# Adaptive projection and Hadamard-quantised feed-forward on one core: written-out start and end, weights in quarters, loop with other lags

## The chip, the core and the metric

The kernel runs on one core of a Trainium2 chip. The time is the device time of one execution in microseconds, and for the kernel before it is the median of three executions, 296.42 us (293.67 to 298.29). The engines are named as the profile names them: PE is TensorE, PEld its weight loads, DVE is VectorE, ACT is ScalarE, POOL is GpSimd, and SP is SyncE, which only issues transfers here. PEq, ACTq and POOLq are the sequencers of those engines.

## What is computed

Sixty-four samples of 64 x 512 are multiplied with a matrix that is picked from 200 by an index. A feed-forward block with ternary weights then runs on the result, and is added to the input. `fwht` is the normalised Walsh-Hadamard transform along the last axis.

```python
def cond(x, conditions, weights):
    return einsum('bct,bcd->bdt', x, weights[conditions])

def act_quant(x):                      # 8 bits, one scale per token
    scale = 127 / clip(max(abs(x), axis=-1, keepdims=True), 1e-5, None)
    return clip(round(x * scale), -127, 127) / scale

def weight_quant(w):                   # ternary, one scale per matrix
    scale = clip(mean(abs(w)), 1e-5, None)
    return clip(round(w / scale), -1, 1) * scale

def hbitlinear(x, w):
    return einsum('bsd,fd->bsf', act_quant(fwht(x)), weight_quant(w))

def reference(x, idx, w_cond, w_up, w_down):
    h = hbitlinear(cond(x, idx, w_cond), w_up)     # 512 -> 1024
    return x + hbitlinear(square(relu(h)), w_down) # 1024 -> 512
```

## The kernel before, in words

Two samples fill the 128 partitions (a pair), and two pairs make a tile, so there are 16 tiles of 256 tokens. All work is written in stages, each a small function of a tile t (and of a half h, k, u or v of it), with its own semaphore waits. For one tile they follow one another like this; the engine stands in brackets.

- `x_outer` [POOL, L340]: the outermost step of the Hadamard transform of x, two halves. `project` [PE, L528]: eight small matmuls with the picked matrices, into the one buffer `y_ps`. `y_high` [ACT, L417] and `y_low` [DVE, L669] split the result in two parts for exact arithmetic.
- `had_z` [PE, L543]: the rest of the transform, into the one buffer `z_ps`. `z_absmax`, `z_floor`, `z_invert` [DVE, L674 to L686] make the scale, `quant_z` [ACT, L423] rounds, `turn_z` [a DMA transpose issued by ACT, L432] turns the tile, and `keep_z` [POOL, L347] keeps the scales.
- `up` [PE, L561], four parts u into two buffers `h_ps`; `relu` [ACT, L439] for each, `square` [ACT, L446] for each pair.
- `g_outer` and `g_inner` [DVE, L693 and L699], two instructions each: two steps of the second transform, SBUF to SBUF. `p_high` [ACT, L452] and `p_low_pool` [POOL, L373] split the result.
- `had_u` [PE, L576], k = 0 and 1, both into the one buffer `u_ps`, so that k = 1 waits until k = 0 has been read. `token_units` [POOL, L352 to L366] works out `kappa`, the floor that `u_floor` needs; `u_absmax`, `u_floor`, `u_invert` [DVE, L713 to L726] make the scale; `quant_u` [ACT, L457] rounds; `turn_u` [DMA transpose from ACT, L464] turns.
- `down` [PE, L586]; `u_unscale` [POOL, L381]; `residual` [DVE, L732] adds x; a store per half.

The order of the work is set by hand. Each engine has a list `step`, in which `run(stage, lag, ...)` means: in step s do this stage for tile s - lag. PE's and DVE's lists reach a lag of 7, ACT's and POOL's a lag of 6. `run_steps` writes the first ten (ACT and POOL: eight) steps out, then loops over two steps at a time up to step 15, and ends with steps in which the stages of tiles past 15 are dropped. So the end of the program keeps the order of the loop.

The weights are prepared in the first steps, by `once(s, stage, ...)`. SP issues the loads, each matrix in two halves, between the loads of x and the gathers of the picked matrices. `weight_abs` sums absolute values, one half on DVE (L624) and one on ACT (L403); `weight_sum` [PE, L504] and `weight_scale` [DVE, L630 to L643] make the scale. Then for each quarter of a matrix: `weight_rint` [ACT, L410] rounds by adding a large constant, `weight_clip` [DVE, L650] limits to -1, 0, 1, `weight_turn` [PE, L515] transposes the low bf16 halves in eight matmuls, `weight_evac` [DVE, L662] takes the constant off while it copies from PSUM. Each gather (L270) waits for POOL's memset of the whole of `w_diag` (L326).

## Time and profile before

| | us |
|---|---|
| median of three executions | 296.42 |
| lowest, highest | 293.67, 298.29 |
| the profiled execution | 297.55 |
| its span, first to last instruction | 295.7 |
| busy: PE, DVE, ACT, POOL | 254.3, 245.7, 185.0, 168.3 |
| mean granted clock of PE, as a share of 2.4 GHz | 0.975 |

The times in the rows below count from the start of the span. Matmuls overlap one another, so the start of one stage to the start of the next tells more of PE than its busy time does.

### The profile page before, as it was taken

The numbers are of one execution on the slowest core, as the hardware profiler recorded it, in microseconds if no ns is written. First come the engines' busy times: TensorE is split into PE (matmuls) and PEld (weight loads), VectorE is DVE, ScalarE is ACT, GpSimd is POOL, SyncE is SP. The second block draws the span as 40 slices with busy tenths as digits, with TensorE's granted clock in tenths as the row PEclk, the third lists the DMA queues.
The fourth block names the chain that finished last, engine by engine and source line by source line (L and its number), as shares of the span: only waits on it lengthen the run. The fifth ranks groups of instructions, "written<-read, shape, count | busy, mean of one in ns | idle before, by whom it ended". The sixth has DMA issues, their size and how long they took to land.

```text
span 295.7 us, 6449 instructions
## 1 busy us (share of the span) xinstructions
PE 254.3 (86%) x1864; PEld 209.1 (71%) x1864; DVE 245.7 (83%) x346; ACT 185.0 (63%) x237; POOL 168.3 (57%) x200
## 2 busy tenths in 40 slices
PE   0277998979899899999899989998999999967863
PEld 0267888859688688888788878887887777635531
DVE  1168799999999988999999999999989898795451
ACT  1068677758577767675867576767676765924310
POOL 8034433595858686656595659574946548474400
PEclk9999899999999999999999999999999999995996
DMA  5585441235385946465664342433343434323262
GB/s 201 206 312 201 121 114 38 88 99 141 98 170 141 162 132 114 144 97 152 104 165 94 90 87 90 88 89 71 106 88 91 90 108 125 64 80 71 92 144 84
DMA packets 67049, 35.16 MB, mean 119 GB/s; under 512 B 57170, under 2 KB 57170, under 8 KB 67026
## 3 DMA queue, kind: packets, MB, share of 16 engines
q10 hardware_dynamic: 51200, 12.59, 24.3%
q1 hardware_dynamic: 15826, 22.29, 22.6%
q8 instruction: 11, 0.18, 0.3%
q14 instruction: 12, 0.10, 0.1%
HBM read 13.89 MB, written 8.39 MB: 75 GB/s over the span
## 4 chain that ended last, share of the span: by engine, by line
DVE 24%; PE 21%; POOL 19%; issue 18%; DMA 6%; ACT 6%; ACTq 2%; SPq 2%; POOLq 1%; DVEq 1%
PE u_ps L576 8%; POOL p_lo L373 8%; DVE g L699 5%; PE o_ps L586 5%; POOL x_half L340 4%; DMA uqT<-uq 4%; DVE u_max L713 3%; PE h_ps L561 3%; PE z_ps L543 3%; POOL u_deq L381 3%; DVE g L693 3%; DVE x_all L650 3%; DVE out_sb L732 2%; DVE z_max L674 2%; ACT uq L457 2%
## 5 line engine op out<-in xcount | busy, mean ns | idle before, releaser
L373 POOL TENSOR_TENSOR p_lo<-g,p_hi 128x1024 fp32r<-128x1024 f32 x32 | 82.8, 2608 | 59.3 <-ACT p_hi L452 51.8
L576 PE MATMUL u_ps<-had_r,p_hi 128*128 128x256 f32 x256 | 65.6, 293 | 11.8 <-ACT uq L457 11.5
L561 PE MATMUL h_ps<-zqT,w_upT 128*128 128x256 f16 x512 | 66.7, 273 | 2.5 <-ACT g L439 2.5
L693 DVE TENSOR_TENSOR g<-g 128x1024 f32<-128x1024 f32 x32 | 66.9, 2099 | 0.2 <-issue 0.2
L586 PE MATMUL o_ps<-w_downT,uqT 128*128 128x512 f16 x256 | 62.2, 387 | 5.1 <-DMA uqT<-uq 4.5
L576 PE MATMUL u_ps<-had_r,p_lo 128*128 128x256 f32 x256 | 63.9, 286 | 0.0
L576 PEld LDWEIGHTS u_ps<-had_r,p_hi 128*128 128x128 f32 x256 | 49.8, 195 | 16.5 <-issue 14.7
L340 POOL TENSOR_TENSOR x_half<-x_all 128x512 f32<-128x512 f32 (+1 forms) x32 | 43.5, 1361 | 21.2 <-DMA x_all<-in_x_dram 14.9
L561 PEld LDWEIGHTS h_ps<-zqT,w_upT 128*128 128x128 f16 x512 | 47.6, 98 | 10.4 <-issue 3.1
L439 ACT ACTIVATE g<-h_ps 128x512 f32<-128x512 f32 x64 | 36.5, 596 | 27.0 <-PE h_ps L561 13.0
L528 PE MATMUL y_ps<-w_diag,x_half 128*128 128x128 f32 (+1 forms) x256 | 38.5, 299 | 15.4 <-DMA w_diag<-in_L_cond_weights_dram 11.1
L713 DVE TENSOR_REDUCE u_max<-u_ps 128x1 f32<-128x1024 f32 x32 | 38.9, 1217 | 13.8 <-PE u_ps L576 13.8
L528 PEld LDWEIGHTS y_ps<-w_diag,x_half 128*128 128x128 f32 x256 | 36.3, 211 | 19.4 <-issue 15.9
L576 PEld LDWEIGHTS u_ps<-had_r,p_lo 128*128 128x128 f32 x256 | 50.0, 195 | 0.0
L699 DVE TENSOR_TENSOR g<-g 128x1024 f32<-128x1024 f32 x32 | 47.1, 1511 | 0.0
L586 PEld LDWEIGHTS o_ps<-w_downT,uqT 128*128 128x128 f16 x256 | 24.7, 99 | 30.9 <-DMA uqT<-uq 5.4
L457 ACT ACTIVATE uq<-u_ps,u_mul 128x1024 f16<-128x1024 f32 x32 | 35.5, 1109 | 17.5 <-DVE u_mul L726 17.4
L452 ACT ACTIVATE p_hi<-g 128x1024 fp32r<-128x1024 f32 x32 | 33.7, 1052 | 8.9 <-DVE g L699 7.8
L423 ACT ACTIVATE zq<-z_ps,z_col 128x512 f16<-128x512 f32 x32 | 22.0, 687 | 26.1 <-DVE z_col L686 25.5
L543 PE MATMUL z_ps<-had_r,y_hi 128*128 128x256 f32 x128 | 34.9, 304 | 2.5 <-ACT zq L423 2.5
L446 ACT ACTIVATE g<-g 128x1024 f32<-128x1024 f32 x32 | 33.6, 1051 | 1.9 <-ACT g L439 0.4
L543 PE MATMUL z_ps<-had_r,y_lo 128*128 128x256 f32 x128 | 33.2, 290 | 0.0
(42 smaller groups left out, 252.8 us busy)
## 6 DMA issues: line engine op xcount, KB each, us to landing
x_all<-in_x_dram SPq DMA_DIRECT2D x16, 512.0 KB, 4.2
out_dram<-out_sb SPq DMA_DIRECT2D x32, 256.0 KB, 2.0
x_all<-in_L_ffn_w_up_dram SPq DMA_DIRECT2D x2, 1024.0 KB, 7.1
x_all<-in_L_ffn_w_down_dram SPq DMA_DIRECT2D x2, 1024.0 KB, 5.9
w_diag<-in_L_cond_weights_dram SPq DMA_DIRECT2D x64, 16.0 KB, 2.4
zqT<-zq ACTq DMA_TRANSPOSE x32, 3.1
uqT<-uq ACTq DMA_TRANSPOSE x32, 3.1
x_all<-in_hadamard_dram SPq DMA_DIRECT2D x1, 256.0 KB, 3.6
```

The lines of the kernel that those rows point to most:

```text
L340: nc.gpsimd.tensor_tensor(x_half[h][:, :, :], xt[:, :, 0, :], xt[:, :, 1, :], (ALU.add, ALU.subtract)[h]).then_inc(s_xh[h], 1)
L373: nc.gpsimd.tensor_tensor(p_lo[par][:, :, i], g[par][:, :, i], p_hi[par][:, :, i].bitcast(FP32), ALU.subtract).then_inc(s_plo[k], 1)
L439: nc.scalar.activation(g[par][:, 2 * u:2 * u + 2, :], h_ps[u % 2][:, :, :], ACT.Relu)\
L457: nc.scalar.activation(uq[k][:, :], u_ps[:, :], ACT.Copy, scale=u_mul[:, k:k + 1])\
L528: mm = nc.tensor.matmul(y_ps[:, l, j * P:(j + 1) * P], x_half[h][:, j, l * P:(l + 1) * P], w_diag[:, bass.ds(t * KP + j, 1), :].rearrange( ...
L543: mm = nc.tensor.matmul(z_ps[:, blk * 256:(blk + 1) * 256], part[par][:, 2 * blk + i, k * P:(k + 1) * P], had_r[:, i, :], start=(i == 0 an ...
L561: mm = nc.tensor.matmul(h_ps[u % 2][:, i, :], w_upT[:, q, f * P:(f + 1) * P], zqT[par][:, q, :], start=(q == 0), stop=(q == TC - 1))
L576: mm = nc.tensor.matmul(u_ps[:, blk * 256:(blk + 1) * 256], part[par][:, 2 * blk + i, k * P:(k + 1) * P], had_r[:, i, :], start=(i == 0 an ...
L586: mm = nc.tensor.matmul(o_ps[k][:, :], uqT[par][k][:, m, :], w_downT[:, m, :], start=(m == 0), stop=(m == FC - 1))
L693: nc.vector.tensor_tensor(g2[:, n, :, :], g[par][:, 0:4, :], g[par][:, 4:8, :], (ALU.add, ALU.subtract)[n]).then_inc(s_g2, 1)
L699: nc.vector.tensor_tensor(p4[par][:, :, n, :], g2[:, :, 0:2, :].rearrange("p h a n -> p h (a n)"), g2[:, :, 2:4, :].rearrange("p h a n -> ...
L713: nc.vector.tensor_reduce(u_max[:, k:k + 1], u_ps[:, :], AX.X, ALU.max, apply_absolute_value=True).then_inc(s_umax[k], 1)
```

## The change

The loop body is reordered on every engine. `once` is gone: `begin(at)` writes out, instruction by instruction, what each engine does before step 5, and `finish(at)` what it does after step 15. The last stages come one step sooner (`down` and `residual` with lag 6), and `up` and `relu` for u = 0 and 1 come with lag 2 in place of 3.

```diff
-            first = (lags + 3) // 2 * 2
-            for s in range(first):
-                step(stages_of(s // 2, s % 2, s), once_in(s))
+            begin(at)
+            first = (lags + 3) // 2 * 2
+            for s in range(BEGIN, first):
+                step(stages_of(s // 2, s % 2, s))
             with eng.Fori(first // 2, TILES // 2) as half:
...
-            for s in range(TILES, TILES + lags):
-                step(stages_of(s // 2, s % 2, s), once_in(s))
+            finish(at)
```

PE's list for a step in the loop, which the prediction goes through:

```diff
-            def step(run, once):
-                run(up, 3, 1)
-                run(down, 7, 1)
-                run(project, 0, 0)
-                run(up, 3, 0)
-                run(had_z, 1, 0)
-                run(had_u, 5, 0)
-                run(up, 3, 2)
-                run(down, 6, 0)
-                run(project, 0, 1)
-                run(up, 3, 3)
-                run(had_u, 5, 1)
-                run(had_z, 1, 1)
+            def step(run):
+                run(down, 6, 0)
+                run(had_u, 5, 0)
+                run(had_z, 1, 0)
+                run(project, 0, 0)
+                run(up, 3, 3)
+                run(down, 6, 1)
+                run(up, 3, 2)
+                run(had_u, 5, 1)
+                run(project, 0, 1)
+                run(up, 2, 0)
+                run(had_z, 1, 1)
+                run(up, 2, 1)
```

PE's written-out start, its first lines, and its whole written-out end, which the prediction adds up:

```diff
+            def begin(at):
+                at(project, 0, 0)
+                at(project, 0, 1)
+                weight_sum(0)
+                at(had_z, 0, 0)
+                at(project, 1, 0)
+                weight_turn(0, 0)
...
+            def finish(at):
+                at(had_u, 11, 0)
+                at(up, 13, 3)
+                at(down, 10, 0)
+                at(had_z, 15, 0)
+                at(up, 13, 2)
+                at(had_u, 11, 1)
+                at(down, 10, 1)
+                at(up, 14, 1)
+                at(up, 14, 0)
+                at(had_u, 12, 0)
+                at(down, 11, 0)
+                at(had_z, 15, 1)
+                at(had_u, 12, 1)
+                at(up, 14, 2)
+                at(up, 14, 3)
+                at(down, 11, 1)
+                at(had_u, 13, 0)
+                at(up, 15, 1)
+                at(up, 15, 0)
+                at(down, 12, 0)
+                at(up, 15, 3)
+                at(up, 15, 2)
+                at(had_u, 13, 1)
+                at(down, 12, 1)
+                at(had_u, 14, 0)
+                at(down, 13, 0)
+                at(had_u, 14, 1)
+                at(down, 13, 1)
+                at(had_u, 15, 0)
+                at(had_u, 15, 1)
...
```

The weights: the up matrix is loaded by ACT's queue, together with the Hadamard matrix, and both matrices come in quarters. The absolute sums are taken by quarters. The rounding writes fp16 straight (the scale is kept 2^24 times larger, so that the values are whole multiples of the smallest fp16 number), and the clip is done by the instruction that empties PSUM. `relu` multiplies the factor back.

```diff
-            def weight_rint(n, u):
+            def weight_round(n, u):
                 act.wait_ge(s_winv[n], 1)
-                part = w_raw[n][:, u * WQ:(u + 1) * WQ]
-                nc.scalar.activation(part, part, ACT.Copy, scale=w_inv[:, n:n + 1], bias=RINT)\
-                    .then_inc(s_wrint[n], 1)
+                nc.scalar.activation(w_int[n][u], w_raw[n][:, u * WQ:(u + 1) * WQ], ACT.Copy,
+                                     scale=w_inv[:, n:n + 1]).then_inc(s_wrint[n], 1)
-            def weight_clip(n, u):
-                dve.wait_ge(s_wrint[n], u + 1)
-                part = w_raw[n][:, u * WQ:(u + 1) * WQ]
-                nc.vector.tensor_scalar(part, part, RINT + 1.0, RINT - 1.0, ALU.min, ALU.max)\
-                    .then_inc(s_wclip[n], 1)
...
-                nc.vector.tensor_scalar(dst, src, float(-BIAS16), None, ALU.add).then_inc(s_wT[n], 1)
+                nc.vector.tensor_scalar(dst, src, UNIT, -UNIT, ALU.min, ALU.max).then_inc(s_wT[n], 1)
```

SP's issues at the start, and POOL's memset, of which only the part of the first two tiles now stands ahead of the first gathers:

```diff
             load_x(0, 0)
-            sp.dma_start(had_f, had).then_inc(s_had, 16)
-            load_weight(0, 0)
             gather_w(0, 0)
-            load_weight(0, 1)
             load_x(0, 1)
             gather_w(0, 1)
-            load_weight(1, 0)
-            load_weight(1, 1)
+            for u in range(4):
+                load_w_down(u)
...
+            act.dma_start(had_f, had).then_inc(s_had, 16)
+            for u in range(4):
+                load_w_up(u)
...
-            nc.gpsimd.memset(w_diag[:, :, :], 0.0).then_inc(s_zero, 1)
+            nc.gpsimd.memset(w_diag[:, 0:2 * KP, :], 0.0).then_inc(s_zero, 1)
...
+            nc.gpsimd.memset(w_diag[:, 2 * KP:PAIRS, :], 0.0).then_inc(s_zero, 1)
```

Three places of the new order. First ACT at its start: what stood there in the kernel before, and what stands there now.

```order
L417 ACT_TABLE_LOAD
L417 ACTIVATE y_hi<-y_ps 128x512
L403 ACTIVATE x_all,w_abs<-x_all 128x2048
L417 ACTIVATE y_hi<-y_ps 128x512
L410 ACTIVATE x_all<-x_all,w_inv 128x1024 x2
L417 ACTIVATE y_hi<-y_ps 128x512
L410 ACTIVATE x_all<-x_all,w_inv 128x1024 x2
```

```order
L509 DMA x_all<-in_hadamard_dram 128x512
L438 DMA x_all<-in_L_ffn_w_up_dram 128x2x512 x4
L459 ACT_TABLE_LOAD
L459 ACTIVATE y_hi<-y_ps 128x512
L446 ACTIVATE x_all,w_abs<-x_all 128x1024 x2
L459 ACTIVATE y_hi<-y_ps 128x512
L452 ACTIVATE x_all<-x_all,w_inv 128x1024 x2
L465 ACTIVATE zq<-z_ps,z_col 128x512
L459 ACTIVATE y_hi<-y_ps 128x512
```

Five DMA issues now stand ahead of ACT's first work, and the first rounding for a token (`zq`) comes right behind the first two quarters. Next DVE in one step of the loop, from the `y_low` of half 1 on: before, and now.

```order
L669 TENSOR_TENSOR y_lo<-y_ps,y_hi 128x512
L713 TENSOR_REDUCE u_max<-u_ps 128x1
L674 TENSOR_REDUCE z_max<-z_ps 128x1
L720 TENSOR_SCALAR u_abs<-u_max,kappa 128x1
L680 TENSOR_SCALAR z_col<-z_max 128x1
L726 RECIPROCAL u_mul<-u_abs 128x1
L732 SCALAR_TENSOR_TENSOR out_sb<-o_ps,u_deq,x_all 128x512
L686 RECIPROCAL z_col<-z_col 128x1
L693 TENSOR_TENSOR g<-g 128x1024
L732 SCALAR_TENSOR_TENSOR out_sb<-o_ps,u_deq,x_all 128x512
L693 TENSOR_TENSOR g<-g 128x1024
```

```order
L869 TENSOR_TENSOR y_lo<-y_ps,y_hi 128x512
L886 RECIPROCAL z_col<-z_col 128x1
L893 TENSOR_TENSOR g<-g 128x1024 x2
L913 TENSOR_REDUCE u_max<-u_ps 128x1
L920 TENSOR_SCALAR u_abs<-u_max,kappa 128x1
L926 RECIPROCAL u_mul<-u_abs 128x1
L899 TENSOR_TENSOR g<-g 128x2x512 x2
L869 TENSOR_TENSOR y_lo<-y_ps,y_hi 128x512
```

All four instructions on `g` now stand close together, with one `u_absmax`, `u_floor`, `u_invert` between them, and both residuals come later. Last ACT at the end of the program, from the `p_high` of tile 14, k = 1, on: before, and now.

```order
L452 ACTIVATE p_hi<-g 128x8x128
L457 ACTIVATE uq<-u_ps,u_mul 128x1024 x2
L464 DMA_TRANSPOSE uqT<-uq 128x8x128
L452 ACTIVATE p_hi<-g 128x8x128
L464 DMA_TRANSPOSE uqT<-uq 128x8x128
L452 ACTIVATE p_hi<-g 128x8x128
L457 ACTIVATE uq<-u_ps,u_mul 128x1024 x2
L464 DMA_TRANSPOSE uqT<-uq 128x8x128 x2
L457 ACTIVATE uq<-u_ps,u_mul 128x1024
L464 DMA_TRANSPOSE uqT<-uq 128x8x128
```

```order
L495 ACTIVATE p_hi<-g 128x8x128
L500 ACTIVATE uq<-u_ps,u_mul 128x1024
L507 DMA_TRANSPOSE uqT<-uq 128x8x128
L495 ACTIVATE p_hi<-g 128x8x128
L500 ACTIVATE uq<-u_ps,u_mul 128x1024
L507 DMA_TRANSPOSE uqT<-uq 128x8x128 x2
L495 ACTIVATE p_hi<-g 128x8x128
L500 ACTIVATE uq<-u_ps,u_mul 128x1024
L507 DMA_TRANSPOSE uqT<-uq 128x8x128
L500 ACTIVATE uq<-u_ps,u_mul 128x1024
L507 DMA_TRANSPOSE uqT<-uq 128x8x128
```

The `p_high` of tile 15 (the second and third `p_hi` rows of each) stood behind the `quant_u` of tile 14, k = 0; now its first half stands ahead of the `quant_u` of tile 14, k = 1, and its second half ahead of the first of tile 15 only.

## Rows read from the trace of the kernel before

**Rows 1.** Stretches: length; busy PE, PEld, DVE, ACT, POOL; PE's clock; DMA share.

```profile
0.00:20.00 20.00, 5.64 (x22) 4.97 (x23) 5.43 (x9) 5.63 (x7) 9.42 (x12) 1.00 0.63 221
20.00:40.00 20.00, 17.90 (x130) 16.65 (x130) 16.81 (x29) 14.77 (x19) 7.59 (x7) 0.91 0.62 198
40.00:60.00 20.00, 18.25 (x171) 16.51 (x170) 19.58 (x30) 14.85 (x22) 8.14 (x6) 1.00 0.22 57
...
72.60:223.60 151.00, 146.25 (x1114) 122.50 (x1115) 141.95 (x200) 107.17 (x141) 102.91 (x120) 1.00 0.51 116
223.60:296.00 72.40, 56.08 (x352) 39.48 (x351) 49.58 (x65) 33.25 (x39) 31.48 (x48) 0.92 0.38 94
```

**Rows 2.** Instructions in order of time, first 23 us; start, length, engine, idle before.

```profile
0.70 3.51 POOL L326 MEMSET w_diag<- 128x4096 f32 x1 [0.29 <-POOLq L802]
...
5.21 4.43 SPq L270 DMA_DIRECT2D w_diag<-in_L_cond_weights_dram  x4
...
11.12 2.04 PE L528 MATMUL y_ps<-w_diag,x_half 128*128 128x128 f32 x8 [11.12 <-DMA w_diag<-in_L_cond_weights_dram]
...
14.67 2.05 PE L528 MATMUL y_ps<-w_diag,x_half 128*128 128x128 f32 x8 [1.50 <-DVE y_lo L669]
...
15.66 1.91 ACT L403 ACTIVATE x_all<-x_all 128x2048 bf16<-128x2048 f32 x1 [1.86 <-DMA x_all<-in_L_ffn_w_up_dram]
...
22.29 0.56 PE L543 MATMUL z_ps<-had_r,y_hi 128*128 128x256 f32 x1
```

**Rows 3.** Groups by line and shape: count, busy, mean ns, idle before.

```profile
L373 POOL TENSOR_TENSOR p_lo<-g,p_hi 128x1024 fp32r<-128x1024 f32 x32 | 82.8, 2608 | 59.3 <-ACT p_hi L452 51.8 <-PE u_ps L576 7.5
...
L650 DVE TENSOR_SCALAR x_all<-x_all 128x1024 f32<-128x1024 f32 x8 | 9.2, 1163 | 0.4 <-ACT x_all L410 0.4
```

**Rows 4.** PE in order of time: `up` for tile 2, tile 3 and tile 13.

```profile
56.69 1.04 PE L561 MATMUL h_ps<-zqT,w_upT 128*128 128x256 f16 x8
...
71.56 1.04 PE L561 MATMUL h_ps<-zqT,w_upT 128*128 128x256 f16 x8
...
222.56 1.04 PE L561 MATMUL h_ps<-zqT,w_upT 128*128 128x256 f16 x8
```

**Rows 5.** The chain that ended last, one step of the loop (200 to 222 us).

```profile
202.27 2.14 PE u_ps L576 x16
204.41 0.96 PE z_ps L543 x8
205.37 0.89 PE h_ps L561 x8
206.26 1.73 PE o_ps L586 x8
...
217.01 2.15 PE u_ps L576 x16
```

**Rows 6.** The same chain, 57 to 72 us: start, length, what.

```profile
57.76 3.39 POOL p_lo L373
...
65.25 3.30 DVE g L699 x2
...
68.57 1.07 ACT p_hi L452
...
72.03 3.39 POOL p_lo L373
```

**Rows 7.** DVE in order of time, at 192 us.

```profile
192.20 3.28 DVE L693 TENSOR_TENSOR g<-g 128x1024 f32<-128x1024 f32 x1
```

**Rows 8.** The chain again, 256 to 296 us.

```profile
268.25 3.75 PE u_ps L576 x16
...
275.01 2.16 PE u_ps L576 x16
...
280.16 2.16 PE u_ps L576 x16
...
285.26 4.64 DMA uqT<-uq
```

510 lines of the change are left out of this document (387 added, 123 removed).

## Prediction

> **What bounds the kernel now.** I read the stretches first. Between 72.6 and 223.6 us PE is busy for 146.25 of 151.0 us and DVE for 141.95, both at the full clock (1.00 of 2.4 GHz), while ACT and POOL have a third of their time left [rows 1]. So there are three kernels in one. There is a start in which little runs, with PE at 5.64 of the first 20 us. There is a middle that PE nearly fills. And there is an end, from 223.6 us on, with PE at 56.08 of 72.4 us and a clock of 0.92. Next the chain that ended last, inside one step of the loop: it stays on PE from 202.27 to 217.01, which is 14.74 us for the twelve stages of a step, one behind the other with no gap [rows 5]. In plain stages that is had_u 1.92 to 2.14, had_z 0.96, up 0.88, down 1.73 and, by subtraction, project 0.89. Ten steps take from 72.6 to 223.6 us (the second `up` of tile 3 ends at 72.6, that of tile 13 at 223.6 [rows 4]), or 15.10 us each. In the loop the most that any order can win is therefore about 0.4 us a step, unless PE's own work shrinks, and it doesn't: the same matmuls are issued.
>
> At the start the chain is a different one. The first gather is issued at 5.21, behind a memset that ends at 4.21, and the first project starts at 11.12 [rows 2]. DVE is busy for 19.58 of the 20 us between 40 and 60 [rows 1]. In the tail I looked for where PE stands still between one had_u and the next, since these share one buffer.
>
> **The change part by part.** The sum is made against the profiled execution, 297.55 us with a span of 295.7, so 1.85 us lie outside the span. It was 1.13 us slower than the median.
>
> *First gather.* The memset ahead of it shrinks to an eighth (about 0.45 of 3.51 us), so the first gather waits for the load of the indices, whose landing no row shows. Before, it came 1.0 us after the memset's end. It can come at 2.2 if the indices are as early as the shorter memset (0.70 + 0.45, and the same 1.0, together), and at 5.21 if they are what it waited for all along. I put it at the middle, 3.7. Four gathers take 4.43 us to issue as before, and the first project would start 1.5 us sooner. Against that, 2 MB of up weights now run beside the gathers from the start, where one half of them was issued only after the gathers. I take 1.0 us of gain (bounds -1 and +3) and start project at 10.1.
> The skill has a rule against this part. The Trainium skill, "DMA: Bandwidth & Descriptors", section "Issuing engines are not separate DMA queues", says that transfers issued by different engines run on the same 16 DMA engines and interleave, and that only sequencer time is saved. Rows 1 show a DMA share of 0.63 over the first 20 us. By that rule alone this part would be worth 0 and the result 1 us later.
>
> *From the first project to the first had_z.* Before, that is 11.12 to 22.29, or 11.2 us [rows 2]. ACT's absolute sum of half a matrix, from 15.66 on, stands ahead of the second y_high, and a third project and the first weight transposes stand ahead of had_z. Now had_z is behind two projects and one tiny matmul. From one project to the next, with y_high and y_low between, it is 14.67 - 11.12 = 3.55 us [rows 2], so two of them make 7.1. had_z starts at 17.2, 5.1 us sooner. The quarter sums on ACT fit inside the wait for the second project.
>
> *The weights.* The clips go: 9.2 us of DVE [rows 3]. They lay where DVE had 36.4 of 40 us busy. The rounding, the transposes and the emptying of PSUM stay, the absolute sums cost the same in more pieces. With DVE relieved, ACT is late next. It was busy for 35.3 us in the first 60 [rows 1]; take off the table load and add 0.6 for four more pieces, and some 34.6 us of it must lie between the first y_high at 12.2 and the last relu ahead of step 5. In 20 to 60 us ACT stood idle for 10.4 of 40; I allow 8 for the shorter stretch. That puts the end of `begin` at 12.2 + 34.6 + 8 = 54.8. Before, the same point is 57.7 (end of the second `up` of tile 2 [rows 4]) plus two weight transposes that are still to come, 58.9. Step 5 has no `down` yet, so PE's content is 14.5 - 3.5 = 11.1; with 0.9 of waits both ups of tile 3 are done at 66.8 to 67.0, against 72.6. Start and step 5 together: 5.6 us gained. The bounds are 1 (only the first gather helps, ACT eats the rest) and 10 (DVE's 9.2 us come through in full).
>
> *The loop.* Ten steps at 15.10. PE's floor is 14.5 to 14.7. The order of PE's list leaves 5.3 us of other stages between the two had_u of a tile, both ways round, where u_absmax, floor, invert, quant_u and their gaps need 280.16 - 275.01 - 2.16 = 2.99 us [rows 8]. So the wait for uq ahead of had_u should go. What may take its place is a ring, visible in rows 6: p_lo ends at 61.15, then POOL's x_half, scales and kappa, then u_floor, g_inner at 65.25 for 3.30, p_hi for 1.07, and two p_lo up to 75.4. The new order has the same ring, with token_units behind one x_outer and both u_unscale on POOL, and u_floor ahead of g_inner on DVE. From the end of one p_low pair to the end of the next I get 4.10 + 3.30 + 1.07 + two gaps of 0.1 + 2 x 2.61 (the mean of p_lo [rows 3]) = 13.9, below 15.1 but not far below. turn_u for k = 0 is issued late in ACT's list, behind both p_high, and down for k = 0 is now PE's first stage of the next step; that leaves about 1 us of slack. I take 15.0 a step, 1.0 us gained over ten, with bounds of 14.7 (4 gained) and 16.0 (9 lost).
> One g_outer takes 3.28 us where p_lo runs beside it [rows 7], and where only short work runs on POOL two g instructions take 3.30 together [rows 6]. The Trainium skill, "SBUF — State Buffer", section "SBUF: two separate sides", says why: a DVE instruction with two SBUF inputs and a GpSimd one that reads SBUF take one port pair in turn, each for its whole length. In the new order the g instructions are early in the step and the p_low pair late, so g meets x_outer instead; by that rule it then waits for at most two x_outer a step. This is the reason why I don't put the loop slower.
>
> *The tail.* At the end of step 15 both kernels have done the same PE work (had_u to tile 10, down to tile 9, ups 0 and 1 of tile 13), so the tails compare from 223.6 on. Before: 295.7 - 223.6 = 72.1 us. After: the had_u run through one buffer, and from one start to the next takes at least 5.15 us (275.01 to 280.16 [rows 8], 2.16 for the matmuls and 2.99 until the buffer has been read). From PE's new list, with 2.0 for had_u itself: 11/0 to 11/1 carries two ups, a down and a had_z, 6.45; then 5.5, 5.15, 5.5, 7.25 (four ups and a down), and four times 5.15. The sum from had_u 11/0 to had_u 15/1 is 50.45. The last had_u to the end of the span was 295.7 - 280.16 = 15.54 and is the same chain in the new order (its transpose alone 4.64 [rows 8]). Together 66.0. I add 1.0 for g and p_lo meeting somewhere: 67.0, a gain of 5.1. What goes is the block at 268.25, where had_u took 3.75 us instead of 2.16 [rows 8]; PE had stood still ahead of it, and the granted clock of the tail is 0.92 [rows 1], so part of it ran at 1.2 GHz instead of 2.4. In the order of before, ACT waits there for the scale of tile 14 with p_high of tile 15 behind it. Bounds: 0 (each wait comes back elsewhere) and 6.5.
>
> *Sum.* 5.6 + 1.0 + 5.1 = 11.7 us. Span 284.0, execution 285.85, and 1.13 less for the median: 284.7 us.
>
> **The rivals.**
> *More than forecast.* The loop runs at PE's content, 14.7 (4 us instead of 1), and the DVE relief comes through, 8 instead of 5.6. For it: DVE is the fullest engine from 40 to 60 us, at 98%, and ACT has a quarter of that time left. Against it: ACT's sum above. Time 284.7 - 3 - 2.4 = 279.3.
> *The start gives little.* ACT is the bound there, its transposes are issued between its own work, and PE catches up on nothing; the tail gives half. 1 + 0 + 2.5 = 3.5 gained: 292.9.
> *Slower: the ring kappa, g_inner, p_high, p_low closes.* If the p_low pair and one g_inner are at their long lengths (2 x 3.39 and 3.28 + 1.65, half of the 3.30), it is 4.10 + 4.93 + 1.07 + 0.2 + 6.78 = 17.1 us a step if that happens in each, and about a half less above 15.1 if in every other. It decides from 15.1 on. I price it at 16.6, where it costs 1.5 us times ten, 15 us, against 10.7 gained at the ends: 296.4 + 4.3 = 300.7. For it: this ring is on the chain already. Against it: p_low no longer meets g.
> *It doesn't do what it says.* The ends wait for landings (the last transpose, 4.64 us, the gathers), which no order shortens; this is the second rival with 0 from the tail as well, and is counted in it.
>
> **How the numbers follow.** Forecast 0.58, more 0.20, little 0.15, slower 0.07. The forecast's own range is 280 to 289. I take the whole range from 275 to 292. Faster than 290.5 is over 2% faster, which is about what a measurement of this kernel can tell from no change: nearly all of the first, all of the second, a fifth of the third, 0.80. Slower by over 2% (302.3) is half of the ring's case at most, 0.04. The rest, 0.16, is within 2%.
>
> **What would show it.** First project near 10.1 and first had_z near 17.2; ACT over 80% busy from 20 to 50 us; ups of tile 3 done by 67; steps of 15.0; had_u starts in the tail 5.15 apart for the last five, at full clock. The forecast is wrong if steps take over 15.5, if p_lo again meets g in the loop, or if the stretch between had_u 13/1 and 15/0 has PE waiting for p_lo.

## The result and the profile after

| us | before | changed |
|---|---|---|
| median (executions) | 295.62 (4) | 311.6 (4) |
| lowest, highest | 293.67, 298.29 | 308.4, 314.84 |
| profiled execution, its span | 297.55, 295.7 | 308.4, 306.3 |
| start, to the second `up` of tile 3 | 72.6 | 69.35 |
| ten steps of the loop | 151.0 | 156.1 |
| tail | 72.1 | 80.8 |

The changed kernel is slower: the ratio is 1.0484, with a 95% interval of 1.0349 to 1.062. The forecast was 284.7 us, so the prediction was wrong by 27 us and in the sign. Start, loop and tail came out at 69.4, 156.1 and 80.8 us where 67.0, 150 and 67.0 were forecast. The start is better than before and the other two parts are worse. Some executions are slow ones, among them two of the four of the changed kernel (314.84 and 313.08 us), and the ratios and the gains below leave them out, so that the gains count from 309.26 us, the median of the other two (308.4 and 310.11), and not from 311.6.

The profiled execution of the kernel before took 297.55 us, where the medians of the later comparisons are 294.8 to 295.12. In its start the granted clock is 0.91 between 20 and 40 us [rows 1]. In the trace of experiment 3, which has the same start, it is 1.00 there, and the second `up` of tile 3 ends at 71.28 instead of 72.6. So of the 3.2 us by which the start seems better, about 1.3 belong to that one execution.

The stretches of the changed kernel, with the columns of [rows 1] (length; busy PE, PEld, DVE, ACT, POOL; PE's granted clock; DMA share; GB/s). The first three are start, loop and tail. The others are the single steps of the loop, cut where `down` of k = 0 starts on PE.

```profile
0.00:69.40 69.40, 48.90 (x389) 45.21 (x390) 40.34 (x77) 44.21 (x62) 32.77 (x34) 0.98 0.53 161
69.40:225.50 156.10, 147.32 (x1121) 122.90 (x1121) 131.71 (x199) 105.15 (x141) 110.04 (x121) 0.99 0.53 108
225.50:306.30 80.80, 58.66 (x354) 41.33 (x352) 47.08 (x68) 34.20 (x40) 31.57 (x48) 0.91 0.35 88
...
84.08:98.58 14.50, 14.50 (x113) 12.30 (x113) 13.81 (x20) 10.64 (x15) 11.82 (x13) 1.00 0.59 135
98.58:114.60 16.02, 14.66 (x115) 12.20 (x112) 13.63 (x21) 10.89 (x16) 11.95 (x15) 1.00 0.61 121
114.60:133.21 18.61, 16.34 (x115) 12.74 (x113) 12.68 (x21) 10.54 (x15) 10.65 (x13) 0.91 0.61 103
133.21:150.84 17.63, 14.64 (x114) 12.19 (x112) 12.69 (x20) 10.52 (x15) 10.98 (x13) 1.00 0.66 108
150.84:167.60 16.76, 14.66 (x114) 12.20 (x112) 12.68 (x21) 10.53 (x15) 10.65 (x13) 1.00 0.67 114
167.60:182.09 14.49, 14.49 (x114) 12.29 (x112) 12.68 (x21) 10.53 (x15) 10.52 (x13) 1.00 0.44 91
```

Read down the length. Some steps take 14.49 or 14.50 us, and in those PE is busy for all of it. Four steps in the middle take 16.02 to 18.61 us, and PE's busy time does not explain them (14.64 to 14.66 in three, 16.34 in the one where the clock was 0.91). DVE, ACT and POOL did no more work there than in the steps around them. So this is a wait that comes and goes. The DMA share stands out: 0.61 to 0.67 in the slow steps, and 0.44 in the first quick one behind them, though 0.59 in the quick one ahead. The share alone does not decide it.

The page's groups tell what PE waited for. These are busy time and mean ns of one, then the idle time ahead and what ended it.

```profile
L366 POOL TENSOR_TENSOR p_lo<-g,p_hi 128x1024 fp32r<-128x1024 f32 x32 | 75.3, 2368 | 71.7 <-ACT p_hi L495 71.6
L705 PE MATMUL h_ps<-zqT,w_upT 128*128 128x256 f16 x512 | 70.0, 285 | 10.2 <-issue 9.6
...
L730 PE MATMUL o_ps<-w_downT,uqT 128*128 128x512 f16 x256 | 62.6, 390 | 11.9 <-DMA uqT<-uq 10.9
...
L893 DVE TENSOR_TENSOR g<-g 128x1024 f32<-128x1024 f32 x32 | 40.4, 1297 | 2.3 <-ACT g L489 1.4
```

`down` stood for 10.9 us because the transposed `uq` had not landed, and `up` for 9.6 us. Meanwhile the part of the change that takes load off DVE did work: `g_outer` (L893) takes 1297 ns in the mean, where its mean before was 2099 (L693) and one beside p_lo took 3.28 us [rows 7], and p_lo itself is at 2368 ns against 2608 [rows 3].

**The loop.** First what SP issues around one slow step, 98 to 107.5 us: start, length of the issue, queue, transfer.

```profile
98.07 0.93 SPq L282 DMA_DIRECT2D out_dram<-out_sb  x2
99.75 0.41 SPq L254 DMA_DIRECT2D x_all<-in_x_dram  x1
101.57 4.97 SPq L267 DMA_DIRECT2D w_diag<-in_L_cond_weights_dram  x4
```

And the chain that ended last, in the same stretch: start, length, what.

```profile
99.44 6.98 DMA uqT<-uq
...
106.47 1.90 PE o_ps L730 x8
...
114.90 8.46 DMA uqT<-uq
```

ACT issues the transpose for k = 1 at 99.44, and 0.31 us later SP issues the load of x for a later pair, 512 KB. The transpose lands after 6.98 us, and PE, which reached `down` for k = 1 at about 105.1, starts it at 106.47. The next one meets its load in the same way (114.90 and 115.15) and takes 8.46 us. Those of the two steps after take 9.17 and 8.29. Each of the four lands 0.2 to 0.3 us behind the load that it met. PE stands idle ahead of `down` for k = 1 for 1.36, 2.27, 2.99 and 2.10 us, 8.7 in all, and the one step at a clock of 0.91 has 1.7 us more of PE's own time; together that is about what the loop has too much. The last load of x is issued at 151.38, and from the next step on the steps are back at 14.49.

**The tail.** The chain that ended last, 236 to 270 us.

```profile
236.12 4.17 issue
240.29 3.44 PE h_ps L705 x16
...
254.77 1.90 PE o_ps L730 x8
...
258.57 3.31 issue
261.88 3.57 PE h_ps L705 x16
...
268.19 1.75 PE h_ps L705 x16
```

The rows called "issue" hold no cause, so one goes to ACT's own rows for the same moments. Start, length, engine, transfer or instruction, and in brackets the idle time before.

```profile
227.83 0.69 ACT L465 ACTIVATE zq<-z_ps,z_col 128x512 f16<-128x512 f32 x1 [0.94 <-DVE z_col L886]
...
236.94 1.24 ACTq L474 DMA_TRANSPOSE zqT<-zq  x1
238.28 1.11 ACT L500 ACTIVATE uq<-u_ps,u_mul 128x1024 f16<-128x1024 f32 x1 [0.90 <-issue]
...
247.39 1.11 ACT L500 ACTIVATE uq<-u_ps,u_mul 128x1024 f16<-128x1024 f32 x1 [7.05 <-DVE u_mul L926]
...
251.39 1.25 ACTq L507 DMA_TRANSPOSE uqT<-uq  x1
251.56 0.67 ACT L465 ACTIVATE zq<-z_ps,z_col 128x512 f16<-128x512 f32 x1
```

`zq` of tile 14 is rounded by 228.5 and its transpose is issued at 236.94, behind a row of other work; `up` waits for it from 236.12 to 240.29. `uq` of tile 11, k = 1 is rounded by 239.4 and its transpose is issued at 251.39, for a `down` that could have started at about 252.5 and starts at 254.77. In ACT's list this transpose stands behind a `quant_u` of tile 12 that had itself stood for 7.05 us, until the `had_u` that PE started at 243.49, behind the first stall, had given its scale. The third is `zq` of tile 15 (251.56), whose transpose is issued at 258.62, and `up` starts at 261.88. PE stands still for 4.17, 2.2 and 3.31 us in the three, and behind the first and the last of them the matmuls are slow too: the same sixteen `up` matmuls take 3.44 and 3.57 us behind such a stall, and 1.75 at 268.19. From `had_u` 11/0 to `had_u` 15/1 it is 67.2 us against the 50.45 forecast (225.47 to 292.67), and from the last one to the end 13.6.

**The start.** Rows of SP's queue and of PE, first 20 us.

```profile
3.02 4.45 SPq L267 DMA_DIRECT2D w_diag<-in_L_cond_weights_dram  x4
...
12.28 2.05 PE L671 MATMUL y_ps<-w_diag,x_half 128*128 128x128 f32 x8 [12.28 <-DMA w_diag<-in_L_cond_weights_dram]
15.83 2.04 PE L671 MATMUL y_ps<-w_diag,x_half 128*128 128x128 f32 x8 [1.50 <-DVE y_lo L869]
...
19.38 0.55 PE L687 MATMUL z_ps<-had_r,y_hi 128*128 128x256 f32 x1 [1.28 <-DVE y_lo L869]
```

The gathers are issued 2.2 us sooner than before [rows 2], and `project` starts 1.16 us later (12.28 against 11.12). Each of the following two distances is 3.55 us, as the forecast had it, so the first `had_z` came 2.9 us sooner than the 22.29 of [rows 2], and not 5.1. In seven other traces with this start `project` starts at 11.51 to 11.80, and in two others with the start of before at 11.13 and 11.24; it is later in all of them, by 0.3 to 1.2 us.

### The profile page after: what moved, and what is told of

Same layout as the page of the kernel before. It is cut to its first block, busy times and chain, and to the rows that moved or that the text cites. A ratio compares the mean times of both kernels' runs of the same rounds, so it can differ in the third digit from the quotient of the medians.

```text
span 306.3 us, 6517 instructions
## 1 busy us (share of the span) xinstructions
PE 254.9 (83%) x1860; PEld 209.4 (68%) x1860; DVE 219.1 (72%) x342; ACT 183.6 (60%) x241; POOL 174.4 (57%) x201
## 4 chain that ended last, share of the span: by engine, by line
PE 43%; DMA 16%; issue 11%; POOL 8%; DVE 8%; SPq 5%; ACTq 4%; ACT 4%; POOLq 0%; DVEq 0%
PE o_ps L730 12%; PE u_ps L720 12%; DMA uqT<-uq 12%; PE h_ps L705 9%; PE y_ps L671 5%; PE z_ps L687 4%; ACTq L474 3%; POOL p_lo L366 3%; DVE u_max L913 2%; SPq L267 2%; SPq L264 2%; POOL x_half L333 2%; DMA w_diag<-in_L_cond_weights_dram 2%; POOL u_deq L374 2%; DMA zqT<-zq 1%
## 5 line engine op out<-in xcount | busy, mean ns | idle before, releaser
L366 POOL TENSOR_TENSOR p_lo<-g,p_hi 128x1024 fp32r<-128x1024 f32 x32 | 75.3, 2368 | 71.7 <-ACT p_hi L495 71.6
L705 PE MATMUL h_ps<-zqT,w_upT 128*128 128x256 f16 x512 | 70.0, 285 | 10.2 <-issue 9.6
L720 PE MATMUL u_ps<-had_r,p_hi 128*128 128x256 f32 x256 | 68.4, 304 | 8.1 <-POOL p_lo L366 5.2
L730 PE MATMUL o_ps<-w_downT,uqT 128*128 128x512 f16 x256 | 62.6, 390 | 11.9 <-DMA uqT<-uq 10.9
L705 PEld LDWEIGHTS h_ps<-zqT,w_upT 128*128 128x128 f16 x512 | 50.6, 102 | 21.6 <-issue 11.0
L481 ACT ACTIVATE g<-h_ps 128x512 f32<-128x512 f32 x64 | 37.4, 593 | 18.7 <-PE h_ps L705 18.5
L671 PE MATMUL y_ps<-w_diag,x_half 128*128 128x128 f32 (+1 forms) x256 | 36.8, 290 | 13.8 <-DMA w_diag<-in_L_cond_weights_dram 12.3
L899 DVE TENSOR_TENSOR g<-g 128x1024 f32<-128x1024 f32 x32 | 45.8, 1467 | 0.0
L671 PEld LDWEIGHTS y_ps<-w_diag,x_half 128*128 128x128 f32 x256 | 33.8, 205 | 14.3 <-issue 14.2
L893 DVE TENSOR_TENSOR g<-g 128x1024 f32<-128x1024 f32 x32 | 40.4, 1297 | 2.3 <-ACT g L489 1.4
L495 ACT ACTIVATE p_hi<-g 128x1024 fp32r<-128x1024 f32 x32 | 33.6, 1054 | 13.6 <-DVE g L899 11.7
L932 DVE SCALAR_TENSOR_TENSOR out_sb<-o_ps,u_deq,x_all 128x512 f32<-128x512 f32 x32 | 23.9, 750 | 18.2 <-PE o_ps L730 15.1
```

The lines of the kernel that those rows point to most:

```text
L366: nc.gpsimd.tensor_tensor(p_lo[par][:, :, i], g[par][:, :, i], p_hi[par][:, :, i].bitcast(FP32), ALU.subtract).then_inc(s_plo[k], 1)
L481: nc.scalar.activation(g[par][:, 2 * u:2 * u + 2, :], h_ps[u % 2][:, :, :], ACT.Relu, scale=1.0 / UNIT)\
L671: mm = nc.tensor.matmul(y_ps[:, l, j * P:(j + 1) * P], x_half[h][:, j, l * P:(l + 1) * P], w_diag[:, bass.ds(t * KP + j, 1), :].rearrange( ...
L705: mm = nc.tensor.matmul(h_ps[u % 2][:, i, :], w_upT[:, q, f * P:(f + 1) * P], zqT[par][:, q, :], start=(q == 0), stop=(q == TC - 1))
L720: mm = nc.tensor.matmul(u_ps[:, blk * 256:(blk + 1) * 256], part[par][:, 2 * blk + i, k * P:(k + 1) * P], had_r[:, i, :], start=(i == 0 an ...
L730: mm = nc.tensor.matmul(o_ps[k][:, :], uqT[par][k][:, m, :], w_downT[:, m, :], start=(m == 0), stop=(m == FC - 1))
```

## The experiments

Theory L (loop): the transpose of k = 1, which has little slack now that `down` comes a step sooner, is drawn out by the load of x beside it. Its rivals were the gathers that SP issues next, a ring through ACT and POOL, and the lag itself. The half about the slack did not hold (experiment 3). Theory T (tail): three transposes stand too late in ACT's list. Its rival was that other waits come in their place. The times of the kernel before stood at 294.8 to 295.12 in these comparisons.

**1. Loop: the load of x behind the gathers.**

```diff
                 for par in range(2):
-                    load_x(half + AHEAD, par)
                     gather_w(half + AHEAD, par)
+                    load_x(half + AHEAD, par)
                     store(half, par)
```

> The changed kernel; in SP's loop of loads and stores, the four gathers of a tile are issued before its load of x instead of after it, so the 512 KB load goes out some 6 us later. In the changed kernel the steps from 98 to 165 us took 16.0 to 18.6 us, and each had a load of x issued 0.25 us behind the transpose turn_u (k = 1), which then landed in 7 to 9 us instead of 3.1. Theory (the x load beside the transpose, and down one stage earlier than before has no slack for it): that transpose lands in 3 to 4 us again, all steps take 14.5 to 15, 8 to 11 us less, about 301 us. Rival (the gathers' small packets hold the transpose up): it still lands in over 6 us, no gain, 311. Rival (the first passes of the loop are slow for another reason, such as code loading): no gain, with landings short.

Measured: 299.24 (296.73 to 300.52), 1.0123 [1.0077, 1.0169] against before, and so 10.0 us less than the 309.26 of the changed kernel (the 12.4 that later expectations name counts from 311.6). What SP issues at the same place, in this kernel:

```profile
98.73 0.92 SPq L282 DMA_DIRECT2D out_dram<-out_sb  x2
101.77 4.70 SPq L267 DMA_DIRECT2D w_diag<-in_L_cond_weights_dram  x4
106.82 0.42 SPq L254 DMA_DIRECT2D x_all<-in_x_dram  x1
```

And its stretches, again start, loop and tail:

```profile
0.00:70.00 70.00, 48.81 (x388) 44.68 (x388) 40.52 (x77) 44.42 (x62) 32.99 (x34) 0.98 0.53 160
70.00:215.80 145.80, 145.23 (x1121) 122.73 (x1121) 135.97 (x199) 104.58 (x140) 113.46 (x121) 1.00 0.48 115
215.80:297.70 81.90, 61.33 (x352) 43.33 (x352) 47.11 (x68) 34.57 (x41) 31.95 (x48) 0.87 0.36 87
```

Ten steps take 145.8 us with PE busy for 145.23. The loop is then 5.2 us faster than before, and nothing of the tail is mended. Between 95 and 170 us the profile gives the time from issue to landing of the `uqT` transposes, least, median and most; in the changed kernel

```profile
DMA to landing us min/median/max: 3.1/3.6/9.2
```

and in this one

```profile
DMA to landing us min/median/max: 3.0/3.5/4.3
```

The four gathers go out at the same moment as in the changed kernel (101.77 here, 101.57 there), while the transpose of k = 1 is on its way (99.89 to 104.16), and it lands in 4.3 us at the most. So it is not the gathers, and the order of the twelve stages has no ring that holds the steps above 14.6 us.

**2. Loop: the load of x waits until the transpose has landed.** Another way to the same end, with the order of the issues as it was.

```diff
                 for par in range(2):
+                    landed = sp.snap(16 * (2 * half + par) + 16)
+                    sp.wait_ge(s_uqT[1], landed)
                     load_x(half + AHEAD, par)
```

> The changed kernel; in the same loop SP waits, before each load of x and its gathers, until the transpose turn_u (k = 1) of that step has landed. Theory: all landings near 3.2 us, steps 14.5 to 15 us, 8 to 11 us less, about 301, as with the other order of load and gathers. If the gathers are what slows the transpose, this gains as much and the other order gains nothing. If neither gains, transfers aren't the cause.

Measured: 299.8 (299.61 to 300.61), 1.0172 [1.0096, 1.0249]. The load is now issued at 104.49, steps are 14.49, and the transposes land in 3.1 to 4.1 us. The wait holds the gathers back as well, where experiment 1 had moved only the load. Two unlike edits that both part the load from the transpose give the same time.

**3. The kernel before, with the meeting forced on it.** SP waits for the last scale ahead of a rounding, so that the load goes out beside the transpose.

```diff
                 for par in range(2):
+                    rounded = sp.snap(2 * half + par + 2)
+                    sp.wait_ge(s_umul[0], rounded)
                     load_x(half + AHEAD, par)
```

> The kernel before; in the same loop SP waits, before each load of x, for the scale u_mul (k = 0), which also lets ACT go on to the transpose turn_u (k = 1), so that load and transpose start together in the kernel before too. Theory (the meeting costs only where down has no slack): that transpose lands in 6 to 9 us, but down for k = 1 comes a step later here, so the time stays within 1% of 295.6. Rival (a transpose and a load that meet cost several us in any order): 4 to 11 us slower.

Measured: 295.71 (294.32 to 298.03), 1.0047 [1.0012, 1.0081]. The row of landings of the same stretch:

```profile
DMA to landing us min/median/max: 3.0/4.7/6.5
```

The transposes are drawn out here too (3.0/3.1/6.6 in the kernel before, where it was one of them), and the time grows by 0.5% only. The theory put that down to lag 7, with which `down` for k = 1 would have a step to spare. The trace shows otherwise: first ACT's issue of the transpose, then PE, with the idle time and what ended it in brackets.

```profile
108.46 1.28 ACTq L466 DMA_TRANSPOSE uqT<-uq  x1
...
112.69 1.05 PE L563 MATMUL h_ps<-zqT,w_upT 128*128 128x256 f16 x8
...
114.78 1.90 PE L588 MATMUL o_ps<-w_downT,uqT 128*128 128x512 f16 x8 [1.04 <-DMA uqT<-uq]
```

In the order of before `turn_u` for k = 1 stands a step later too (lag 6), and `down` for k = 1 stands near the head of PE's next step. So from the issue of this transpose to the moment when PE wants it there are 5.3 us (108.46 to 113.74), and 5.2 to 6.2 in the other steps that meet a load. In the changed kernel it is 5.7 to 6.2 (99.44 to 105.11 in the first). The slack is about the same in both, and a landing that takes longer is paid for in both: this one took 6.26 us and cost 1.04, the next took 6.54 and cost 0.38, the other three stayed at 5.0 or below and cost nothing. The sum of 1.4 us is what the ratio shows. In the profile of the kernel before itself one transpose took 6.57 us, and `down` waited 1.25 for it.

So this run does not show that it takes a lost lag besides the meeting. It shows a milder meeting: 6.5 us at the most against 9.2. Here the load goes out 0.06 to 0.19 us behind the transpose, and the last store was issued 2.7 us ahead or earlier; in the changed kernel the load is 0.24 to 0.60 us behind, and two stores of 256 KB have been issued 0.4 to 1.4 us ahead. Which of these makes the difference was not tried.

**4. Loop: more slack for k = 1.** `down` for k = 1 behind `had_u` for k = 1, and the residuals of the two halves in the other order.

```diff
                 run(up, 3, 3)
-                run(down, 6, 1)
                 run(up, 3, 2)
                 run(had_u, 5, 1)
+                run(down, 6, 1)
                 run(project, 0, 1)
...
-                run(residual, 6, 1)
+                run(residual, 6, 0)
...
-                run(residual, 6, 0)
+                run(residual, 6, 1)
```

> The changed kernel; in the loop body alone PE does down (k = 1) behind had_u (k = 1) instead of two stages ahead of it, and DVE takes the residual of k = 1 last, that of k = 0 first. The load of x still meets the transpose, but down comes 2.8 us later in the step, and the stores with it. Theory (a slow transpose costs what it exceeds the slack of down): the four long steps, 16.0, 18.6, 17.6 and 16.8 us against 14.5, lose 2 to 3 us each, 6 to 10 us in all, if transpose and load still meet: 301 to 306. If the later stores part the two, the whole 12 us come back: 299. Rival (slack isn't the matter, the slow landing holds ACT's or SP's queue up): no gain, 311.

Measured: 301.38 (300.87 to 304.6), 1.0254 [1.0201, 1.0307]. The load and the transpose still meet, but in the other order: the load is issued 0.3 to 1.0 us ahead (98.91 and 99.18, then 114.99 and 115.95). The transposes land in 3.0/5.1/6.0 us, those of k = 1 that met a load in 5.0 to 5.5. `down` for k = 1 now comes 9 to 11 us behind its transpose and waits for none. What the loop still loses is ahead of `down` for k = 0: the stores come later too, the first of them now 0.7 us behind the transpose of k = 0, which lands in 5.0 to 6.0 us while loads go on and in 4.3 to 4.8 when only the stores are left. Of `down`, between 85 and 225 us, the profile says how long PE sat idle until what, and how often:

```profile
  DMA uqT<-uq: 3.7, 4
```

Start and loop end at 219.46, against 225.47 in the changed kernel and 215.8 in experiment 1, and the difference to experiment 1 is these 3.7 us. The run changed the slack of k = 1 and the landing times at once, so it does not tell what the slack alone is worth. Parting the two transfers gives more.

**5. Tail: three transposes moved forward in ACT's written-out end.** The loop keeps its fault.

```diff
                 at(square, 13, 0)
+                at(turn_z, 14, 1)
                 at(quant_u, 11, 0)
...
-                at(turn_z, 14, 1)
                 at(quant_u, 11, 1)
                 at(p_high, 12, 1)
+                at(turn_u, 11, 1)
                 at(quant_u, 12, 0)
...
-                at(turn_u, 11, 1)
+                at(turn_z, 15, 1)
                 at(quant_u, 12, 1)
...
-                at(turn_z, 15, 1)
```

> The changed kernel; three transposes are moved forward in ACT's written-out end: turn_z of tile 14 (k = 1) to the second place, turn_u of tile 11 (k = 1) behind the p_high that follows its quant_u, turn_z of tile 15 (k = 1) right behind its quant_z. In the changed kernel PE stood still for 4.2, 4.0 and 3.3 us ahead of the up of tile 14, the down of tile 11 and the up of tile 15, each until one of these had landed, though the rounded values had been ready 6 to 12 us. Theory (PE waits for transposes that ACT issues late): the last 80.8 us fall to 68 to 72, 9 to 13 us less, about 301. Rival (ACT as a whole is late, or kappa and the ring behind it sets the pace): 0 to 3 us less.

Measured: 299.16 (297.57 to 302.25), 1.0118 [1.0017, 1.022], so 10.1 us less than the changed kernel (299.13 against 309.26), and 9.0 in the profiled spans. Its tail in one row, from its 226.6 on:

```profile
226.60:297.30 70.70, 56.24 (x355) 40.50 (x352) 48.22 (x68) 34.23 (x41) 31.97 (x48) 0.94 0.41 101
```

70.7 us instead of 80.8, and 2.4 us of it are PE's own busy time (58.66 to 56.24), at a clock of 0.94 instead of 0.91. The `had_u` starts are 6.95, 6.02, 5.15, 7.51, 7.55, 5.55, 5.74, 5.96 and 5.15 us apart, so no wait of 4 us came back elsewhere. A few of 0.4 to 2 did, at other places.

**6. Tail: only the first of the three.** The `turn_z` of tile 14 alone.

> The changed kernel; only the first of the three transposes is moved forward, turn_z of tile 14 (k = 1) to the second place of ACT's written-out end. PE stood still for 4.2 us ahead of the up that waits for it. Theory (each late transpose costs its own wait): 4 us less, 307 to 308; the other two make up the rest of the 12.4 us. Rival (PE then reaches the next late transpose sooner, and waits longer there, so that the first alone gives under 1 us): 311.

Measured: 303.73 (301.04 to 313.82), 1.0266 [1.0223, 1.0308]. The median for the gain is 303.38, so this one moved line gives 5.9 of the 10.1 us. The theory had 4, the length of the wait. The wait of 4.17 us and the 1.7 us that the matmuls right behind it took too long (3.44 against 1.75) make 5.9; that sum is an account that fits, not a test. The profile is of the execution of 313.82 us, in which start and loop are 9 us longer, so it is read for the place itself only: from `had_u` 11/1 to `had_u` 12/0, where the first stall was, it is 6.10 us against 11.27, and the stretch from `had_u` 12/1 to 13/1, with the other two stalls, is 20.2 against 21.1. So the rival, that the wait comes back at the next late transpose, did not hold.

**7. Both mends, 1 and 5.**

> The changed kernel with both mends: gathers ahead of the load of x in SP's loop, and the three transposes moved forward in ACT's written-out end. Alone they took 12.4 us (to 299.2) and 12.4 us (to 299.2) off the changed kernel's 311.6. Theory (two separate faults, one in the loop and one in the end): the gains add, 311.6 - 12.4 - 12.4 = 286.8, between 285 and 290, so 2 to 3% faster than before. Rival (both mends shorten the same queue of transposes, so that one takes the other's gain): 293 or more.

Measured: 290.05 (289.14 to 290.62), 0.9813 [0.978, 0.9846].

```profile
0.00:69.60 69.60, 48.89 (x389) 44.80 (x390) 40.27 (x77) 44.17 (x62) 32.72 (x34) 0.98 0.52 161
69.60:215.70 146.10, 144.98 (x1120) 122.61 (x1120) 133.62 (x200) 104.78 (x140) 111.41 (x121) 1.00 0.49 115
215.70:288.00 72.30, 56.17 (x355) 40.45 (x352) 47.97 (x68) 34.57 (x41) 31.94 (x48) 0.95 0.43 99
```

Singly the two give 10.0 and 10.1 us, together 19.2. The theory's sum of 286.8 was made from 311.6; from 309.26 it is 289.2, and 290.05 is within 0.9 us of it, so the two faults are separate as far as two executions of the changed kernel can tell. Two orders of issue, with the same work in them, turn 4.8% slower into 1.9% faster. Against before (the trace of experiment 3 for the start, 71.28, and [rows 1] for the loop) the start gives 1.7 us and the loop 4.9, in sum 1.1 us more than the 5.5 of the ratio. The written-out tail is worth nothing that can be seen even when mended: it took 70.7 to 72.4 us in four traces (experiments 5, 7, 10 and 11), and the order of before took 70.0 to 74.3 in four (before, and experiments 3, 8 and 9).

**8. The new start alone.** `begin` and the new weights as changed, and behind them the loop and the dropped-stage end of before.

> The changed kernel's start (everything ahead of step 5, with the weights in quarters, the fewer passes and the new loads), followed by the loop lists and the dropped-stage end of the kernel before; what the start has done already is left out of step 5. It measures the start alone. From the traces, both ups of tile 3 end at 69.4 us instead of 72.6, so the start theory says 2 to 5 us faster than before, 290.5 to 293.5. Rival (the start gains nothing, since the first project comes later, at 12.3 instead of 11.1, and the loop takes the rest back): 295 or more.

Measured: 294.27 (291.56 to 297.66), 0.9941 [0.9904, 0.9978]. The start by itself is worth 1.3 us by the medians for the gain (293.78 against 295.1) and 1.7 by the ratio, which is less than the 2 to 5 of the theory. In the trace the second `up` of tile 3 ends at 69.24, 2.0 us sooner than the 71.28 of experiment 3.

**9. The weight passes alone.** The kernel before, with the fp16 rounding and the clip in the emptying of PSUM, and nothing else changed.

```diff
-                nc.vector.tensor_scalar(part, part, RINT + 1.0, RINT - 1.0, ALU.min, ALU.max)\
-                    .then_inc(s_wclip[n], 1)
+                pass
...
-                nc.vector.tensor_scalar(dst, src, float(-BIAS16), None, ALU.add).then_inc(s_wT[n], 1)
+                nc.vector.tensor_scalar(dst, src, UNIT, -UNIT, ALU.min, ALU.max).then_inc(s_wT[n], 1)
```

> The kernel before in its own order; only the weight passes are changed: the rounding writes fp16, the clip is done by the instruction that empties PSUM, and the eight clip passes (9.2 us of DVE) are gone. Theory (DVE was what bounded 40 to 60 us): 2 to 6 us faster, 290 to 293.5. Rival (the order written for the clips waits for ACT's roundings at the same places, so nothing comes forward): within 1 us of 295.

Measured: 293.5 (292.35 to 296.0), 0.9964 [0.9935, 0.9994]. DVE sheds 9.2 us of clips, and 1.1 to 1.6 us of it reach the end (by the ratio and by the medians). The first `up` starts at 36.01 against 36.62. DVE was the busiest engine from 40 to 60 us [rows 1] and yet was not what held the others back for most of that time.

**10. The last two quarters of the up weights held back** until the first pair's matrices have landed, on top of 7.

```diff
             act.dma_start(had_f, had).then_inc(s_had, 16)
-            for u in range(4):
-                load_w_up(u)
+            load_w_up(0)
+            load_w_up(1)
+            act.wait_ge(s_wc[0], LOADED)
+            load_w_up(2)
+            load_w_up(3)
```

> The kernel with both mends; ACT issues the last two quarters of the up weights only when the gathers of tile 0 have landed. In the changed kernel the first gather was issued early, yet the first project started at 12.3 us instead of 11.1, while the DMA share of the first 20 us was 0.81 instead of 0.63. Theory (the up weights, 2 MB on ACT's queue, hold the gathers up): the first project comes at 10 to 11 us, and the time falls by 0 to 2 us. Rival (the gathers are late because of the index load or SP's issue): the project stays at 12.3 and the weights' scale comes later, 1 to 3 us slower.

Measured: 288.71 (287.1 to 291.33), 0.979 [0.9743, 0.9838]. PE, first rows:

```profile
9.01 2.05 PE L674 MATMUL y_ps<-w_diag,x_half 128*128 128x128 f32 x8 [9.01 <-DMA w_diag<-in_L_cond_weights_dram]
12.60 2.05 PE L674 MATMUL y_ps<-w_diag,x_half 128*128 128x128 f32 x8 [1.54 <-DVE y_lo L872]
16.94 0.56 PE L651 MATMUL o_ps<-w_abs,ones 128*128 128x4 f32 x2 [2.29 <-ACT x_all L446]
18.15 0.55 PE L690 MATMUL z_ps<-had_r,y_hi 128*128 128x256 f32 x1 [0.65 <-DVE y_lo L872]
```

SP issues its four gathers at 3.01 for 4.45 us, as in the changed kernel (3.02, 4.45), and `project` starts 3.3 us sooner than there, and 2.5 sooner than in experiment 7, where it was 11.51. So it is the weights' load from the other queue that delays the gathers. Part of the gain is lost at once: the held quarters come later, so ACT's absolute sum of the fourth one stands ahead of the second `y_high`, and the first `had_z` comes only 1.2 us sooner than 19.38 (and 0.5 sooner than the 18.61 of experiment 7). The DMA share of the first 20 us is 0.79 here, hardly below the 0.81 of the changed kernel, so the share does not show whether the gathers are held up. The whole kernel is 1.3 us faster than in experiment 7 by the medians, within the spread of the runs.

**11. The first tile ahead of the weights' scale**, on top of 10: `had_z` before `weight_sum` on PE, its scale before the weights' on DVE, and on ACT `y_high` before the fourth absolute sum and the first `quant_z` before the second rounding.

```diff
                 at(project, 0, 1)
-                weight_sum(0)
                 at(had_z, 0, 0)
+                weight_sum(0)
...
-                weight_abs(0, 3)
                 at(y_high, 0, 1)
+                weight_abs(0, 3)
...
```

> The kernel with both mends and the held-back quarters (288.7 us); the first had_z, its scale and its rounding come ahead of the weights' scale on PE, DVE and ACT, so that nothing of tile 0 waits for the sum of the up weights, which held the first had_z at 18.15 us though its input was ready near 16. Theory: had_z starts by 16.5 us and the time falls by 0.5 to 2 us. Rival (the weights' scale is what the first up waits for, and it comes 1 to 2 us later now): 0 to 2 us slower.

Measured: 286.87 (286.04 to 289.68), 0.974 [0.9699, 0.9782]. This is the fastest kernel of the study, 2.6% ahead of the one before. The first `had_z` starts at 17.12. In its profile the first `up` starts no sooner than in experiment 10 (31.75 against 31.57). The step from 10 to 11 is no larger than the spread of the runs, so what each of them gives is not settled.

## Why the prediction was wrong

**What bounds it: right.** The loop is bound by PE. Where nothing disturbs the new order a step takes 14.49 us, below the 15.0 forecast and the 14.7 that was its lower bound.

**The loop: the step that failed is the landing time of `uqT`, taken as given.** The prediction put the loop at 15.0 us a step, 1.0 us gained, and looked at one transpose only: "turn_u for k = 0 is issued late", which "leaves about 1 us of slack". The k that failed was the other one. `turn_u` for k = 1 goes out at 99.44 and `down` for k = 1 could start at about 105.1, so it had 5.7 us, in which a landing of 3.1 fits well. What was not asked is which transfer the new order puts beside it. In the new order the two stores of a step, and SP's load of x behind them, fall on the issue of this transpose (98.07, 99.75 and 99.44), which then needs 7 to 9.2 us. By experiments 1 and 2 this costs 10.3 us of the profiled execution (156.1 to 145.8) and 10 us of the median. So the loop lost 5.1 us where 1.0 was to be gained. The slack was no smaller than before (5.3 us there, by experiment 3); what changed is the landing.

**The rival "slower": the right sign, by a mechanism that was not there.** It put the ring kappa, g_inner, p_high, p_low at 16.6 us a step and 300.7 us in all. The steps were up to 18.6 us, yet in experiment 1, with the ring as it was, they are 14.49. The argument against the ring, that p_low no longer meets g, held: `g_outer` is down to 1.3 us.
The rule of the Trainium skill cited there ("SBUF — State Buffer", section "SBUF: two separate sides") fits these rows: with p_lo elsewhere in the step, `g_outer` fell from a mean of 2.10 us, and 3.28 for one beside p_lo [rows 7], to a mean of 1.30.

**The tail: the step that failed is the sum of 50.45 us.** It was made of two things, PE's content between two `had_u` and the 5.15 us for reading `u_ps`, and took it for granted that every operand is there. Three of PE's operands are transposes that ACT issues, and where they stand in ACT's list was never looked at. The forecast named ACT's waits in the kernel before, and didn't search the new list for the same. They cost 10.1 us (80.8 to 70.7, experiment 5; the tail is 80.1 to 81.9 in the four traces with all three of them and 70.7 to 72.4 in the four without). The rest, 3.7 us above 67.0, are small waits of 0.4 to 2 us between `had_u` starts and a clock of 0.94. Where no such wait stood, the 5.15 was right (5.15, 5.16, 5.32).

**The first gather: wrong sign.** The forecast started `project` at 10.1, and it started at 12.28. The gathers were issued at 3.02, sooner than the 3.7 assumed, and the last of the four landed 5.2 us behind its issue, where this had been 1.8 in the kernel before. What the up weights beside them cost was taken too low. Experiment 10 shows the size: without half of the weights beside them `project` starts at 9.01.
The rule of the Trainium skill that was set against this part ("DMA: Bandwidth & Descriptors", section "Issuing engines are not separate DMA queues") pointed the right way, down from the +1.0 forecast, but it put the part at 0, and the part measured -1.2 us (-0.3 to -1.2 over the traces).

**The start as a whole.** The forecast had the end of `begin` at 54.8 and 12.0 us for step 5. On PE step 5 starts at 57.22 and takes 12.1. Of the 2.4 us in between, 2.2 are the late first `project`, and they are there at the first `had_z` already (19.38 against 17.2). So the sum over ACT fits (ACT is busy for 24.77 of the 30 us from 20 to 50, 83%), and the term that failed is the first gather. The gain came out at 3.2 us of the 5.6 against the profile of before, and at 1.9 against the start of experiment 3. The clips were worth less than their length: since DVE had been busy for 36.4 of 40 us, the upper bound let the 9.2 us through in full and the first rival counted on 8 for the start, and experiment 9 gains 1.1 to 1.6 from taking them out.

With the two faults mended the kernel takes 290.05 us, with the start in order 286.87. The forecast of 284.7 is 2.2 us from what the plan could be brought to, with an order of the first loads that it did not have, and far from what the kernel as written does.

## What to carry to other kernels

When the order of a loop is changed, look up for each operand that comes by DMA when the transfer is issued, which other transfers are now issued within a microsecond of it, and by which events those are set off. A landing time read from the trace of before holds only beside the neighbours it had there. In an in-order list a DMA issue is an instruction like any other: write it right behind the work that makes its data, ahead of anything that can wait, and in a hand-written end go through the issuing engine's list as well as the consumer's. An engine that is 90% busy in some stretch is not by that the one the others wait for; take the work away alone and time it, before adding its length to a gain.
